# The score maxima of two pairs of heads taken in one visit, and two small steps moved to the second step of the experts' stage

## The chip, the cores and the metric

The kernel runs on one core of one Trainium2 chip. The metric is the device time of one execution in microseconds (us). Engines are named as in the profile: PE is TensorE, DVE is VectorE, ACT is ScalarE, POOL is GpSimd, SP issues the large DMAs.

## The reference

For each of 16 inputs x of 256 x 128 the result is `x + scan(xn) + experts(attention(xn))`, with `xn = layernorm(x)`:

```python
# branch one: a depthwise convolution and a state-space recurrence with 16 states
xf = depthwise_conv(xn, conv_w, conv_b)                       # 3 taps
dt = sigmoid(xf @ dt_w.T + dt_b) * (DT_MAX - DT_MIN) + DT_MIN
s  = exp(dt * A) * s + (dt * xf) * b ;  y = sum_d s * c        # along the 256 rows
# branch two: 16 heads of 64, causal attention with q and k scaled to length one
h = layernorm(xn) * g + b ;  q, k, v = h @ Wq, h @ Wk, h @ Wv
attn = softmax(where(causal, l2norm(q) @ l2norm(k).T * 10, -1e9))
h = layernorm((attn @ v) @ Wo) ;  gate = softmax(h @ gate_w + gate_b)
out = layernorm(sum_e gate[e] * (gelu(h @ w1[e] + b1[e]) @ w2[e] + b2[e]))   # 8 experts
```

## The kernel before

All weights stay in SBUF. The inputs go through a software pipeline written out by hand, one loop `body(i)` for each of the engines, which are joined by counting semaphores alone; every engine works through its own list strictly in order. `body(i)` has two stages. The **attention stage** has ten steps `k = 0..9`: scores, exponentials and weighted values of input i, the q, k, v projections of input i+1, the 16 state scans of input i (as far as `SCAN_AT` puts them here), layer norms of inputs i-1, i-2 and i+2. The **experts' stage** has ten steps `m = 0..9`: the output projection of input i, the eight experts of input i-1 (`expert_up`, `gelus`, `expert_down`, `add_expert`), and the preparation of input i+1: q and k are turned (`turn_qk`, eight transposes for two calls), split into a high and a low half (`high` on ACT, `low` on DVE), and a pass over the scores gives each row's maximum for the softmax.

That **max pass** is taken for one pair of heads at a time. On PE `scores_for_max(s, p)` writes four products of 64 rows each (L400, the two heads in the two halves of the array) and then adds the causal mask with four products of 128 rows (L404). On DVE `maxima(s, p)` reduces them with two `tensor_reduce` (L1101). All passes of inputs 1 to 15 use one double bank of PSUM, S2, so the pass of pair p waits until the maxima of pair p-1 are taken; passes stand in steps m = 1 to 8, one in each. `turn_max` (L420) turns four pairs' maxima, `copy_max` (L730) copies them.

PSUM has eight banks: S2, O2 and U2 of two banks each and J[0], J[1]. J takes the projections, `turn_qk`, `turn`, `turn_max` and `step_sizes`.

Other pieces that the change touches: `turn` (L335, L337) turns the normalised input i+2, `g_step(i+2, 6)` makes it (four normalisings, L1010), `g_step` 7 to 9 copy it out of PSUM and split it (L1035, L1036, L1040, L1043). `convolve` (L1175, L1179: three operations) gives `xf`, `step_sizes` (L575) multiplies it by dt_w, `step_tanh` (L767) and `step_inputs` (L1187, L1191) follow. `scan` and `add_state` (L1198, L1208) are one state of the recurrence. `turn_gate` (L523), `o_step` 14 (L1156), `gated_b2` (L529) and `o_step` 15 (L1159) hand the gates of input i-1 from PE to DVE and back twice before the first expert is added. POOL's `units` (L920) scale q and k to length one: four operations follow the last `norm_step` (L1066) in step m = 0, then `x_bias` (L935).

Of the kernel before, what the change touches and what calls it, by code (L numbers as in the profile page):

```python
# [14 lines left out]
P = 128  # L15
# [25 lines left out]
def build(nc, x, a_log, b, c, dt_w, dt_b, conv_w, conv_b, ln_g, ln_b, Wq, Wk, Wv, q_scale, k_scale,  # L41
          Wo, gate_w, gate_b, w1, b1, w2, b2, out):
    ctx = ExitStack()
    with ctx:
# [131 lines left out]
        J = [ctx.enter_context(nc.psum_tensor(f"J{n}", [P, 512], F32)) for n in range(2)]  # L176
# [48 lines left out]
        def max_bank(s, p):  # L225

            return O2 if s == 0 and p % 2 == 1 else S2
# [27 lines left out]
        def step_bank(s):  # L255
            return U[1][:, 0:SEQ] if s == 0 else J[1][:, 0:SEQ]

        TURN_AT = {0: 0, 1: 2, 3: 4, 4: 6}
        MAX_AT = {1 + p: (p,) for p in range(NP)}
# [65 lines left out]
        def _(pe):  # L325
            mm, tr = nc.tensor.matmul, nc.tensor.transpose

            def turn(s):
                pe.wait_ge(g_vec, s * KG + 10)
                if not isinstance(s, int) or s > 0:  # L330
                    pe.wait_ge(t_lo, s * NL - 1)
                if s == 1:
                    pe.wait_ge(mt_done, 1)
                for t in range(T):
                    tr(J[0][:, t * P:(t + 1) * P], xn[:, t, :], ident[:, :])  # L335
                for t in range(T):
                    last = tr(J[0][:, SEQ + t * P:SEQ + (t + 1) * P], z[:, t, :], ident[:, :])  # L337
                last.then_inc(g_tr, 1)
# [29 lines left out]
            def turn_qk(s, n):  # L368
# [6 lines left out]
                elif n < 2:  # L375
                    pe.wait_ge(qk_raw, NJ - 1 + n)
                else:
                    pe.wait_ge(t_lo, s * NL + n - 1)
                for a in range(2):
# [6 lines left out]
            def scores_for_max(s, p):  # L386

                pe.wait_ge(t_hi, s * NL + 2 * (p // 2) + 2)
                if p == 0:
                    from_one(pe, ex_done, s * NP)  # L390
                    from_one(pe, wo_copied, s)
                elif s == 0:
                    from_one(pe, mx_done, 2 * (p - 1))
                else:
                    pe.wait_ge(mx_done, s * 2 * NP + 2 * p)
                bank = max_bank(s, p)
                for t in range(T):
                    for a in range(2):
                        r = slice(a * DH, (a + 1) * DH)
                        mm(bank[:, a, t * P:(2 * t + 1) * P], QTh[r, p, t * P:(t + 1) * P],  # L400
                           KTh[r, p, 0:(t + 1) * P], start=True, stop=False, skip_group_check=True)
                for a in range(2):
# [4 lines left out]

            def turn_max(s, g):
                pe.wait_ge(mx_done, s * 2 * NP + NP * (g + 1))
                if g == 0:  # L410
                    if s == 0:
                        pe.wait_ge(t_lo, NL - 1)
                    elif s < LAST:
                        pe.wait_ge(g_vec, (s + 1) * KG + 12)
                    else:
                        pe.wait_ge(t_lo, (s + 1) * NL - 1)
                else:
                    pe.wait_ge(tanh_done, s + 1)
                for t in range(T):
                    last = tr(J[g][:, t * P:(t + 1) * P],  # L420
# [148 lines left out]
            def step_sizes(s):  # L569
# [3 lines left out]
                else:  # L573
                    pe.wait_ge(t_lo, (s + 1) * NL)
                mm(step_bank(s), dtwT[:, :], xf[:, :], start=True, stop=True).then_inc(dt_ready, 1)  # L575

            def prologue():
# [17 lines left out]
                for n in range(NL):  # L595
                    turn_qk(0, n)
                    if n % 2 == 1:
                        scores_for_max(0, n - 1)
                        scores_for_max(0, n)
# [10 lines left out]
            def body(i, older, old, new, newer):  # L610
# [24 lines left out]
                for m in range(NE + 2):  # L635
# [7 lines left out]
                    if new:  # L643
                        for p in MAX_AT.get(m, ()):
                            scores_for_max(i + 1, p)
# [17 lines left out]
                    if newer and m == 6:  # L663
                        turn(i + 2)
                    if new and m == 7:
                        step_sizes(i + 1)
# [15 lines left out]
        def _(act):  # L682
# [45 lines left out]
            def copy_max(s, g):  # L728
                act.wait_ge(mt_ready, 2 * s + g + 1)
                fn(mT[:, g, :], J[g][:, 0:SEQ], ACT.Copy).then_inc(mt_done, 1)  # L730
# [95 lines left out]
            def body(i, older, old, new, newer):  # L826
# [43 lines left out]
                for m in range(NE + 2):  # L870
# [10 lines left out]
                    if new and m > 0 and m in TURN_AT:  # L881
                        high(i + 1, TURN_AT[m])
                        high(i + 1, TURN_AT[m] + 1)
                    if old and 1 <= m < NE:
                        gelus(i - 1, m)
                    if new and m == 8:
                        step_tanh(i + 1)
# [106 lines left out]
        def _(dve):  # L994
# [18 lines left out]
            def g_step(s, n):  # L1013
# [18 lines left out]
                elif n == 7:  # L1032
                    dve.wait_ge(g_tr, s + 1)
                    from_one(dve, c_vec, (s - 1) * KC + 3)
                    V.tensor_copy(xnT[:, 1:SEQ + 1], J[0][:, 0:SEQ]).then_inc(g_vec, 1)  # L1035
                    V.tensor_scalar(hT[:, :], J[0][:, SEQ:2 * SEQ], lng, lnb, ALU.mult, ALU.add  # L1036
# [283 lines left out]
            G_AT = {0: (0, 1), 3: (2,)}  # L1320
            O_AT = {1: (5,), 3: (6, 7), 4: (8,), 5: (9, 10), 9: (12, 13)}
            O_LAST_AT = {2: (0, 1, 2), 3: (5,), 4: (6, 7, 8), 5: (9, 10), 7: (12, 13), 8: (14,), 9: (15,)}
            SCAN_AT = {1: (0,), 3: (1,), 5: (2,), 6: (3,), 8: (4,), 9: (5,)}
# [128 lines left out]
```

## Time and profile before

| | |
|---|---|
| median of three runs | 1122.25 us (1120.18 to 1125.5) |
| the profiled execution | 1120.17 us, its span 1118.4 us |
| PE busy | 1075.0 us, 96% |
| DVE busy | 959.6 us, 86% |
| ACT busy | 778.9 us, 70% |
| POOL busy | 277.7 us, 25% |
| granted TensorE clock, mean | 0.986 of full speed |

The span runs from the first instruction to the last. The time of the execution has 1.8 us outside it. One input takes 66.2 us in the middle of the run: the attention stage about 28.6 us and the experts' stage about 37.6 us. Matmuls overlap in the pipeline, so a matmul's own duration (0.27 us and the like) is longer than the distance from one start to the next (0.11 us).

### The profile page before, as it was taken

The page shows a single profiled execution, that of the slowest core. Times are in us where ns is not written, and L with a number is a line of the kernel's source. Part 1 is how long each engine was busy: PE and PEld are TensorE (multiplying, and loading weights), DVE is VectorE, ACT ScalarE, POOL GpSimd, SP SyncE. Part 2 cuts the span into 40 slices and gives each one's busy share as a digit, 9 for nine tenths or more (in the row PEclk, how much of TensorE's full clock was granted, in tenths as well). Part 3 has the DMA queues.
Part 4 walks back from the last instruction along what each step waited for, and adds up shares of the span by engine and source line. Part 5 has one row for each costly group of instructions (what it writes and reads, how often), then busy time and mean ns, then how long its engine had stood idle before and what let it go on. Part 6 is the DMA issues. An engine that isn't in the chain of part 4 may idle for free.

```text
span 1118.4 us, 27576 instructions
## 1 busy us (share of the span) xinstructions
PE 1075.0 (96%) x10435; PEld 912.2 (82%) x10435; DVE 959.6 (86%) x2543; ACT 778.9 (70%) x1772; POOL 277.7 (25%) x328
## 2 busy tenths in 40 slices
PE   4877999999999999999999999999999999999997
PEld 1664888888888888888888888888888888888897
DVE  8988798898988989898898989889898888988763
ACT  5873948668595876859677594867759587685653
POOL 2340314224031231404123140412403132140200
PEclk9995999999999999999999999999999999999999
DMA  7010000000000000000000000000000000000000
GB/s 210 7 39 10 2 11 7 1 16 1 11 7 11 6 2 16 1 11 6 6 11 2 11 7 11 6 1 16 2 11 6 11 7 6 6 6 1 7 2 10
DMA packets 18722, 14.60 MB, mean 13 GB/s; under 512 B 2408, under 2 KB 16160, under 8 KB 18592
## 3 DMA queue, kind: packets, MB, share of 16 engines
q1 hardware_dynamic: 17680, 12.76, 3.8%
q8 instruction: 84, 1.38, 0.5%
q14 instruction: 46, 0.38, 0.1%
q10 hardware_dynamic: 912, 0.09, 0.1%
HBM read 10.75 MB, written 2.10 MB: 11 GB/s over the span
## 4 chain that ended last, share of the span: by engine, by line
PE 89%; DVE 4%; issue 3%; ACT 2%; POOL 1%; SPq 0%; DMA 0%; POOLq 0%; DVEq 0%; ACTq 0%
PE O L565 19%; PE O L468 14%; PE S L484 5%; PE U L547 5%; PE U L548 5%; PE U L549 5%; PE J L382 5%; PE S L449 4%; PE J L343 4%; PE U L449 4%; PE S L404 4%; PE J L344 3%; PE J L345 3%; PE S L400 3%; PE O L475 2%
## 5 line engine op out<-in xcount | busy, mean ns | idle before, releaser
L777 ACT ACTIVATE hid<-U,b1c 128x256 f32<-128x256 f32 x512 | 200.5, 474 | 174.8 <-PE U L549 174.7
L565 PE MATMUL O<-w2s,hid 128*128 128x128 f32 x2048 | 251.1, 276 | 0.0
L565 PEld LDWEIGHTS O<-w2s,hid 128*128 128x128 f32 x2048 | 238.6, 192 | 2.9
L928 POOL TENSOR_SCALAR_AFFINE_SELECT P<-P 128x512 f32<-128x512 f32 x128 | 85.0, 664 | 618.6 <-ACT P L750 618.5
L468 PEld LDWEIGHTS O<-Vx,P 128*128 128x128 f32 x1536 | 188.0, 192 | 30.2 <-issue 14.3
L468 PE MATMUL O<-Vx,P 128*128 128x66 f32 x1536 | 188.6, 273 | 3.6 <-POOL P L928 2.0
L1198 DVE TENSOR_TENSOR_SCAN st<-aexp,u 128x256 f32<-128x256 f32 x256 | 178.8, 698 | 0.4 <-issue 0.3
L920 POOL TENSOR_TENSOR raw<-raw,nr 128x512 f32<-128x512 f32 x124 | 132.8, 1097 | 134.9 <-DVE nr L1066 134.9
L1208 DVE SCALAR_TENSOR_TENSOR y<-st,bc,y 128x256 f32<-128x256 f32 x240 | 133.5, 556 | 8.5
L547 PE MATMUL U<-h2h,w1h 128*128 128x256 f16 x480 | 130.9, 273 | 0.0
L549 PE MATMUL U<-h2h,w1l 128*128 128x256 f16 x480 | 130.9, 273 | 0.0
L548 PE MATMUL U<-h2l,w1h 128*128 128x256 f16 x480 | 130.9, 273 | 0.0
L1101 DVE TENSOR_REDUCE mxn<-S 128x2 f32<-128x256 f32 x248 | 125.7, 549 | 0.7 <-PE S L404 0.3
L762 ACT ACTIVATE aexp<-dt,negA 128x256 f32<-128x256 f32 x256 | 117.2, 518 | 0.0
L1169 DVE SCALAR_TENSOR_TENSOR acc<-O,gate,acc 128x128 f32<-128x128 f32 x240 | 73.1, 346 | 43.5 <-PE O L565 39.2
L1047 DVE TENSOR_REDUCE ssq<-sq 128x8 f32<-128x512 f32 x128 | 86.3, 674 | 0.5 <-ACT sq L701 0.4
L699 ACT ACTIVATE raw<-J 128x512 f32<-128x512 f32 x128 | 76.7, 599 | 3.1 <-PE J L345 3.1
L701 ACT ACTIVATE sq<-J 128x512 f32<-128x512 f32 x128 | 78.1, 610 | 0.0
L343 PE MATMUL J<-wh,hTh 128*128 128x512 f16 x188 | 72.8, 387 | 3.9 <-DVE hTl L1043 1.9
L344 PE MATMUL J<-wh,hTl 128*128 128x512 f16 x188 | 72.0, 383 | 0.0
L345 PE MATMUL J<-wl,hTh 128*128 128x512 f16 x188 | 71.9, 383 | 0.0
L382 PE MATMUL J<-ident,raw 128*128 128x128 f32 x512 | 68.6, 278 | 3.3 <-DVE raw L1075 2.1
(204 smaller groups left out, 2048.0 us busy)
## 6 DMA issues: line engine op xcount, KB each, us to landing
xin<-in_L_attn_x SPq DMA_DIRECT2D x16, 128.0 KB, 2.1
xres<-in_L_attn_x SPq DMA_DIRECT2D x16, 128.0 KB, 2.3
hid<-in_L_ffn_w SPq DMA_DIRECT2D x2, 1024.0 KB, 6.5
out_dram<-fin SPq DMA_DIRECT2D x16, 128.0 KB, 1.8
raw<-in_L_ffn_Wq SPq DMA_DIRECT2D x1, 512.0 KB, 4.7
raw<-in_L_ffn_Wk SPq DMA_DIRECT2D x1, 512.0 KB, 6.4
raw<-in_L_ffn_Wv SPq DMA_DIRECT2D x1, 512.0 KB, 7.4
wos<-in_L_ffn_Wo SPq DMA_DIRECT2D x1, 512.0 KB, 11.4
```

The source lines that it names most:

```text
L343: mm(dst, hi, wh[:, w0:w0 + 512], start=True, stop=False)
L382: last = tr(J[n % 2][:, (a * T + t) * P:(a * T + t + 1) * P], raw[:, chunk(t, kind, half), c0:c0 + P], ident[:, :])
L468: last = mm(dst, P32[:, p % 3, a, c0:c0 + P], Vx[:, kb, 2 * p + a, :], start=(kb == 0), stop=(kb == t))
L547: mm(dst, w1h[:, f:f + P], hi[:, :], start=True, stop=False)
L548: mm(dst, w1h[:, f:f + P], lo[:, :], start=False, stop=False)
L549: last = mm(dst, w1l[:, f:f + P], hi[:, :], start=False, stop=True)
L565: last = mm(O[e % 2][:, t * P:(t + 1) * P], hid[:, e % 2, m, t * P:(t + 1) * P], w2s[:, e * FC + m, :], start=(m == 0), stop=(m == FC - 1))
L777: fn(hid[:, e % 2, f % FC, :], U[q % 2][:, m * SEQ:(m + 1) * SEQ], ACT.Gelu_apprx_tanh, bias=b1c[:, f:f + 1], scale=1.0 / WS).then_inc(gel ...
L920: nc.gpsimd.tensor_tensor(group, group, nr[:, j * 8:(j + 1) * 8].unsqueeze(2).broadcast_to([P, 8, DH]), ALU.mult).then_inc(unit, 1)
L1101: V.tensor_reduce(mxn[:, t, g, hh:hh + DH + 2:DH + 1], max_bank(s, p)[:, :, t * P:(2 * t + 1) * P], AX.X, ALU.max, negate=True).then_inc(m ...
L1198: V.tensor_tensor_scan(st[:, d % 2, :], aexp[:, d, :], u[:, :], 0.0, ALU.mult, ALU.add).then_inc(scan_done, 1)
L1208: V.scalar_tensor_tensor(y[:, s % 2, :], st[:, d % 2, :], bc[:, d:d + 1], y[:, s % 2, :], ALU.mult, ALU.add).then_inc(y_done, 1)
```

## The change

- `scores_for_max` now takes two pairs in one call: products of pair p, products of pair p+1, masks of p, masks of p+1. The even pair lies in S2 and the odd one in J2 (the two J banks, now one tensor), for input 0 in O2. Calls stand in steps m = 2, 5, 6 and 7; `maxima` of both pairs follow in the same steps.
- `turn(i+2)` and `step_sizes(i+1)` move on PE from steps 6 and 7 to step 1, ahead of the expert's products, and use S2 where they used J. The first max pass waits until both have been read out of S2. `step_tanh` moves to step 1 on ACT. `turn_max` of the first half moves to U[0].
- `turn_qk` calls 4 and 5 (step 3) wait for the first two pairs' maxima, since these are now in the J banks.
- On DVE `g_step(i+2, 6)` moves to step k = 8 of the attention stage and the three `convolve` to k = 9; `g_step` 7 to 9 move to step m = 1. State 4's scan moves from k = 8 to k = 9, state 5's from k = 9 to m = 0. In m = 0 the scans of states 6 and 7 now stand behind `low` and the `norm_step`s, before them up to now.
- In body 0 attention takes seven scans where it took ten, and the experts' stage nine where it took six.

```diff
@@ -173,7 +173,8 @@
         O = [O2[:, n, :] for n in range(2)]
-        J = [ctx.enter_context(nc.psum_tensor(f"J{n}", [P, 512], F32)) for n in range(2)]
+        J2 = ctx.enter_context(nc.psum_tensor("J2", [P, 2, 512], F32))
+        J = [J2[:, n, :] for n in range(2)]
         U2 = ctx.enter_context(nc.psum_tensor("U2", [P, 2, 512], F32))
@@ -224,7 +225,14 @@
-            return O2 if s == 0 and p % 2 == 1 else S2
+            return S2 if p % 2 == 0 else O2 if s == 0 else J2
+
+        def turn_bank(s):
+            return J[0] if s < 2 else S2[:, 1, :]
+
+        def turned_max_bank(s, g):
+
+            return (U[0] if g == 0 and s > 0 else J[g])[:, 0:SEQ]
@@ -253,10 +261,10 @@
         def step_bank(s):
-            return U[1][:, 0:SEQ] if s == 0 else J[1][:, 0:SEQ]
+            return U[1][:, 0:SEQ] if s == 0 else S2[:, 0, 0:SEQ]
         TURN_AT = {0: 0, 1: 2, 3: 4, 4: 6}
-        MAX_AT = {1 + p: (p,) for p in range(NP)}
+        MAX_AT = {2: 0, 5: 2, 6: 4, 7: 6}
@@ -327,14 +335,15 @@
                 pe.wait_ge(g_vec, s * KG + 10)
-                if not isinstance(s, int) or s > 0:
-                    pe.wait_ge(t_lo, s * NL - 1)
                 if s == 1:
+                    pe.wait_ge(t_lo, NL - 1)
                     pe.wait_ge(mt_done, 1)
-                for t in range(T):
-                    tr(J[0][:, t * P:(t + 1) * P], xn[:, t, :], ident[:, :])
-                for t in range(T):
-                    last = tr(J[0][:, SEQ + t * P:SEQ + (t + 1) * P], z[:, t, :], ident[:, :])
+                elif s > 1:
+                    pe.wait_ge(ex_done, (s - 1) * NP)
+                for t in range(T):
+                    tr(turn_bank(s)[:, t * P:(t + 1) * P], xn[:, t, :], ident[:, :])
+                for t in range(T):
+                    last = tr(turn_bank(s)[:, SEQ + t * P:SEQ + (t + 1) * P], z[:, t, :], ident[:, :])
                 last.then_inc(g_tr, 1)
@@ -376,6 +385,8 @@
                     pe.wait_ge(t_lo, s * NL + n - 1)
+                if s > 0 and n in (4, 5):
+                    pe.wait_ge(mx_done, s * 2 * NP + 4)
                 for a in range(2):
@@ -383,41 +394,56 @@
-            def scores_for_max(s, p):
-
-                pe.wait_ge(t_hi, s * NL + 2 * (p // 2) + 2)
-                if p == 0:
-                    from_one(pe, ex_done, s * NP)
-                    from_one(pe, wo_copied, s)
-                elif s == 0:
-                    from_one(pe, mx_done, 2 * (p - 1))
-                else:
-                    pe.wait_ge(mx_done, s * 2 * NP + 2 * p)
+            def max_products(s, p):
                 bank = max_bank(s, p)
...
                            KTh[r, p, 0:(t + 1) * P], start=True, stop=False, skip_group_check=True)
+
+            def max_masks(s, p):
+                bank = max_bank(s, p)
                 for a in range(2):
...
+            def scores_for_max(s, p):
+
+                pe.wait_ge(t_hi, s * NL + p + 2)
+                if s == 0:
+                    from_one(pe, mx_done, 2 * (p - 1))
+                    max_products(0, p)
+                    from_one(pe, mx_done, 2 * p)
+                elif p == 0:
+                    pe.wait_ge(ex_done, s * NP)
+                    pe.wait_ge(wo_copied, s)
+                    pe.wait_ge(tanh_done, s + 1)
+                    if s < LAST:
+                        pe.wait_ge(g_vec, (s + 1) * KG + 12)
+                    pe.wait_ge(t_lo, s * NL + 4)
+                    max_products(s, p)
+                else:
+                    pe.wait_ge(t_lo, s * NL + NL)
+                    pe.wait_ge(mx_done, s * 2 * NP + 2 * p)
+                    max_products(s, p)
+                max_products(s, p + 1)
+                max_masks(s, p)
+                max_masks(s, p + 1)
+
             def turn_max(s, g):
...
                         pe.wait_ge(t_lo, NL - 1)
-                    elif s < LAST:
-                        pe.wait_ge(g_vec, (s + 1) * KG + 12)
                     else:
-                        pe.wait_ge(t_lo, (s + 1) * NL - 1)
-                else:
-                    pe.wait_ge(tanh_done, s + 1)
-                for t in range(T):
-                    last = tr(J[g][:, t * P:(t + 1) * P],
+                        from_one(pe, gelu_done, (s - 1) * NE * FC)
+                else:
+                    pe.wait_ge(t_lo, (s + 1) * NL)
+                for t in range(T):
+                    last = tr(turned_max_bank(s, g)[:, t * P:(t + 1) * P],
                               mxn[:, t, g, :], ident[:, :])
@@ -571,7 +597,7 @@
                 else:
-                    pe.wait_ge(t_lo, (s + 1) * NL)
+                    pe.wait_ge(wo_copied, s)
                 mm(step_bank(s), dtwT[:, :], xf[:, :], start=True, stop=True).then_inc(dt_ready, 1)
@@ -596,7 +622,6 @@
                         scores_for_max(0, n - 1)
-                        scores_for_max(0, n)
                     if n == 1:
@@ -640,9 +665,12 @@
                         turn_gate(i - 1, (i + 1) * NP)
-                    if new:
-                        for p in MAX_AT.get(m, ()):
-                            scores_for_max(i + 1, p)
+                    if new and m == 1:
+                        step_sizes(i + 1)
+                    if newer and m == 1:
+                        turn(i + 2)
+                    if new and m in MAX_AT:
+                        scores_for_max(i + 1, MAX_AT[m])
                     if old and 1 <= m < NE:
@@ -660,10 +688,6 @@
                         gated_b2(i)
-                    if newer and m == 6:
-                        turn(i + 2)
-                    if new and m == 7:
-                        step_sizes(i + 1)
                     if not old and m == NE + 1:
@@ -727,7 +751,7 @@
                 act.wait_ge(mt_ready, 2 * s + g + 1)
-                fn(mT[:, g, :], J[g][:, 0:SEQ], ACT.Copy).then_inc(mt_done, 1)
+                fn(mT[:, g, :], turned_max_bank(s, g), ACT.Copy).then_inc(mt_done, 1)
@@ -881,10 +905,10 @@
                         high(i + 1, TURN_AT[m] + 1)
+                    if new and m == 1:
+                        step_tanh(i + 1)
                     if old and 1 <= m < NE:
                         gelus(i - 1, m)
-                    if new and m == 8:
-                        step_tanh(i + 1)
                 if new:
@@ -1032,8 +1056,8 @@
                     from_one(dve, c_vec, (s - 1) * KC + 3)
-                    V.tensor_copy(xnT[:, 1:SEQ + 1], J[0][:, 0:SEQ]).then_inc(g_vec, 1)
-                    V.tensor_scalar(hT[:, :], J[0][:, SEQ:2 * SEQ], lng, lnb, ALU.mult, ALU.add
+                    V.tensor_copy(xnT[:, 1:SEQ + 1], turn_bank(s)[:, 0:SEQ]).then_inc(g_vec, 1)
+                    V.tensor_scalar(hT[:, :], turn_bank(s)[:, SEQ:2 * SEQ], lng, lnb, ALU.mult, ALU.add
                                     ).then_inc(g_vec, 1)
@@ -1317,11 +1341,11 @@
             E_AT = {0: (0, 1, 2), 2: (5, 6), 3: (7,)}
-            G_AT = {0: (0, 1), 3: (2,)}
+            G_AT = {0: (0, 1), 3: (2,), 8: (6,)}
             O_AT = {1: (5,), 3: (6, 7), 4: (8,), 5: (9, 10), 9: (12, 13)}
             O_LAST_AT = {2: (0, 1, 2), 3: (5,), 4: (6, 7, 8), 5: (9, 10), 7: (12, 13), 8: (14,), 9: (15,)}
-            SCAN_AT = {1: (0,), 3: (1,), 5: (2,), 6: (3,), 8: (4,), 9: (5,)}
-            FIRST_SCAN_AT = {1: (0, 1), 2: (2,), 3: (3,), 4: (4,), 5: (5,), 6: (6,), 7: (7,), 8: (8,), 9: (9,)}
+            SCAN_AT = {1: (0,), 3: (1,), 5: (2,), 6: (3,), 9: (4,)}
+            FIRST_SCAN_AT = {k: (k - 1,) for k in range(1, 8)}
@@ -1353,6 +1377,9 @@
                             g_step(i + 2, n)
+                    if new and k == 9:
+                        for n in range(3):
+                            convolve(i + 1, n)
                     if k != 6:
@@ -1364,46 +1391,42 @@
                         add_expert(i - 1, m - 2)
+                    if new and m in MAX_AT:
+                        maxima(i + 1, MAX_AT[m])
+                        maxima(i + 1, MAX_AT[m] + 1)
                     if old and m == 0:
-                        for d in (6, 7):
-                            scan(i, d)
-                            add_state(i, d)
+                        scan(i, 5)
+                        add_state(i, 5)
                     if new and m == 0:
...
                             norm_step(i + 1, 1, n)
+                    if old and m == 0:
+                        for d in (6, 7):
+                            scan(i, d)
+                            add_state(i, d)
                     if old and 2 <= m <= NE:
...
                         add_state(i, m + 7)
-                    if not old and 1 <= m <= 6:
-                        scan(i, m + 9)
-                        add_state(i, m + 9)
+                    if not old and m <= 8:
+                        scan(i, m + 7)
+                        add_state(i, m + 7)
                     if old and m == 1:
...
                         low(i + 1, TURN_AT[m] + 1)
-                    if new:
-                        for p in MAX_AT.get(m, ()):
-                            maxima(i + 1, p)
+                    if newer and m == 1:
+                        g_step(i + 2, 7)
+                        g_step(i + 2, 8)
                     if old and m == 1:
...
                         add_state(i, m + 7)
-                    if newer and m == 5:
-                        g_step(i + 2, 6)
-                    if new and m == 2:
-                        convolve(i + 1, 0)
-                    if new and m == 6:
-                        convolve(i + 1, 1)
-                        convolve(i + 1, 2)
+                    if newer and m == 1:
+                        g_step(i + 2, 9)
                     if not old and m == 3:
                         split_w1(1, 0, 1)
-                    if newer and m == 7:
-                        g_step(i + 2, 7)
-                        g_step(i + 2, 8)
-                    if newer and m == 8:
-                        g_step(i + 2, 9)
                     if new and m == 9:
```

## Rows read from the trace of the kernel before

**Rows 1.** The page, part 1: busy time and share of the span.
```profile
PE 1075.0 (96%) x10435; PEld 912.2 (82%) x10435; DVE 959.6 (86%) x2543; ACT 778.9 (70%) x1772; POOL 277.7 (25%) x328
```

**Rows 2.** Busy time by stretch; after POOL: granted clock, DMA share, GB/s.
```profile
18.00:42.00 24.00, 16.14 (x128) 8.85 (x127) 22.66 (x58) 17.70 (x35) 5.05 (x5) 1.00 0.47 135
81.00:106.00 25.00, 16.52 (x115) 10.95 (x116) 22.28 (x50) 5.82 (x10) 0.89 (x2) 0.50 0.04 11
464.63:502.21 37.58, 37.58 (x357) 33.64 (x356) 33.38 (x79) 22.25 (x53) 5.19 (x5) 1.00 0.03 9
502.21:530.82 28.61, 28.61 (x299) 23.03 (x299) 25.36 (x80) 25.54 (x58) 12.09 (x15) 1.00 0.02 6
```

**Rows 3.** Timeline of PE around step m = 2: start, us, what.
```profile
472.17 0.71 PE L529 MATMUL O<-b2s,gateT 8*128 8x128 f32 x4
472.80 2.05 PE L565 MATMUL O<-w2s,hid 128*128 128x128 f32 x16
474.79 0.34 PE L400 MATMUL S<-KTh,QTh 64*128 64x128 f16 x4
475.06 0.40 PE L404 MATMUL S<-maskb,identb 128*128 128x128 bf16 x4
475.29 0.27 PE L547 MATMUL U<-h2h,w1h 128*128 128x256 f16 x1
```

**Rows 4.** The chain that ended last, steps 6 and 7: start, us, what.
```profile
495.09 0.22 PE J L335 x2
...
499.23 0.43 PE J L575 x2
```

**Rows 5.** DVE's busy time in short stretches, each one piece of work.
```profile
459.91:461.63 1.72, 1.68 (x3) 1.00 0.00 0
463.61:464.73 1.12, 1.08 (x3) 1.00 0.00 0
466.97:468.35 1.38, 1.38 (x4) 1.00 0.00 0
468.35:468.99 0.64, 0.57 (x4) 1.00 0.00 0
472.12:473.05 0.93, 0.93 (x3) 1.00 0.00 0
474.97:475.50 0.53, 0.53 (x3) 1.00 0.00 0
490.31:491.33 1.02, 1.02 (x5) 1.00 0.00 0
494.01:494.95 0.94, 0.91 (x3) 1.00 0.00 0
497.71:498.89 1.18, 1.15 (x4) 1.00 0.00 0
```

**Rows 6.** Timeline of DVE, step k = 9 to step m = 1.
```profile
463.61 0.68 DVE L1198 TENSOR_TENSOR_SCAN st<-aexp,u 128x256 f32<-128x256 f32 x1
...
468.80 0.19 DVE L1066 SCALAR_TENSOR_TENSOR nr<-nw,ny 128x32 f32<-128x32 f32 x1
470.37 0.42 DVE L1156 COPY gateT<-O 128x256 f32<-128x256 f32 x1 [1.38 <-PE O L523]
```

**Rows 7.** Timeline of POOL: the first in the attention stage, the others m = 0.
```profile
66.11 2.42 POOL L920 TENSOR_TENSOR raw<-raw,nr 128x512 f32<-128x512 f32 x2
74.84 4.54 POOL L920 TENSOR_TENSOR raw<-raw,nr 128x512 f32<-128x512 f32 x4 [6.31 <-DVE nr L1066]
...
469.07 4.04 POOL L920 TENSOR_TENSOR raw<-raw,nr 128x512 f32<-128x512 f32 x4 [7.64 <-DVE nr L1066]
```

**Rows 8.** Timeline of DVE in body 0, beside the first two of rows 7.
```profile
66.71 0.99 DVE L1198 TENSOR_TENSOR_SCAN st<-aexp,u 128x256 f32<-128x256 f32 x1
67.73 1.08 DVE L1208 SCALAR_TENSOR_TENSOR y<-st,bc,y 128x256 f32<-128x256 f32 x1
...
75.40 1.08 DVE L1208 SCALAR_TENSOR_TENSOR y<-st,bc,y 128x256 f32<-128x256 f32 x1
```

## The prediction, made before the changed kernel was run

> **What bounds the kernel now.** I read the page first: PE is busy for 96% of the span, DVE for 86% [rows 1]. Then the windows of one input in the middle of the run: PE is busy in every moment of both stages, at full clock; DVE has 4.2 us to spare in the experts' stage and 3.3 us in the attention stage [rows 2]. So PE's own list sets the period of 66.2 us (37.58 + 28.61), and anything that PE no longer issues comes off it, once for each input. But DVE is only 11% behind, so the question of this change is whether DVE's new order still has each thing ready when PE asks. The third view is the timeline of the steps m = 0 to 3, where the change moves most.
>
> **What the change removes on PE.** In the timeline the last of the 16 matmuls of L565 starts at 472.80 + 2.05 - 0.28 = 474.57, the pass begins at 474.79, its masks at 475.06, the next product at 475.29 [rows 3]. Full-height matmuls start every 0.11 us, so going to 64-row products costs 0.22 - 0.11 = 0.1 us. The four products are two side-by-side couples of 128 and 256 columns: by PE's pace 0.055 + 0.11 = 0.165 us, but the masks come after 0.27 us, so going back costs 0.1 us as well. A single pass takes 0.50 + 0.1 = 0.6 us, two in one call 0.1 + 0.165 + 0.27 + 2 x 0.23 = 1.0 us. A joined call saves one way out and one way back, 0.21 us. Four for each input: **0.84 us**. The Trainium skill ("TensorEngine Tiling (Array Packing)", Key Properties) says that changing the tiling mode drains TensorE; it gives no figure, and the sum goes by the rows.
>
> `turn` (0.22 + 0.22 us) and `step_sizes` (0.43 us) [rows 4] only move: 0.87 us leave steps 6 and 7 and come into step 1. The same for every moved DVE operation. Nothing else on PE changes, no DMA does, and ACT (59% busy in this stage [rows 2]) only gets `step_tanh` earlier; its table load moves off the end, which PE did not wait for. With all else hidden, the 14 bodies that have an expert's stage and a next input (1 to 14) give 14 x 0.84 = 11.8 us.
>
> **DVE: is everything in time?** Prices, from one start to the next [rows 5]: scan with its add 1.12, the same beside POOL's `units` 1.72; a pair of `low` 1.38; the three norm steps 0.64; two reductions 0.93; `add_expert` 0.53; `g_step` 6 1.02; the last two convolutions 0.94, all three 1.34 with a first of `o_step` 14's size; `g_step` 7 and 8 1.18; `g_step` 9, `o_step` 14 and 15 about 0.35 each (copies of that size).
>
> Step k = 8: the four normalisings take the place of a scan that ran beside POOL. Uncovered they take 1.02 us, and if POOL holds them up by as much as it did the scan and its add (1.72 - 1.12), 1.6 us against 1.72: the same end within 0.2 us. After that DVE begins at 463.61 [rows 6]. Up to now scans 5, 6, 7 (3.36 us) stood before `low`; now convolutions and scans 4, 5 (1.34 + 2.24 = 3.58 us): `low` is 0.22 us later, at 467.2, and PE asks for it only behind eight transposes and the 32 matmuls of `output`, at 464.63 + 40 x 0.11 = 469.0. No cost.
>
> Then the norm steps end, and scans 6 and 7 follow where DVE sat idle for 1.38 us before `o_step` 14 at 470.37 [rows 6]. They begin at 467.2 + 1.38 + 0.57 = 469.15. Without any hindrance they end at 471.4.
>
> **The hindrance.** The last norm step releases POOL's four units, 4.04 us back to back [rows 7]. Up to now DVE had nothing with two SBUF inputs in that time. In body 0 it had one scan there: POOL's four then took 4.54 us in place of 4.04, and the add behind the scan 1.08 us in place of 0.48; in the attention stage a scan and an add that met the two units of 66.11 took 0.99 and 1.08 in place of 0.68 and 0.48 [rows 7, 8]. The numbers fit one reading: a DVE operation that meets a running unit does nothing until that unit ends, and then the next unit waits for it (the first unit ends at 66.11 + 1.04, the scan 0.55 us later at 67.70; the second ends at 68.53, the add 0.28 us later at 68.81). Played out from 469.15: scan 6 is first and holds unit 1 up until about 469.63 (of the 0.5 us that POOL lost in body 0 I give the scan 0.3, the add 0.2); unit 1 to 470.67, the add ends 470.95; unit 2 to 471.88, scan 7 ends 472.43 (0.88 late); unit 3 to 473.26, its add ends 473.54. So add, scan and add are late by 0.6 + 0.88 + 0.6 = **2.1 us**, and `o_step` 14 begins at 473.46. Bounds: from below nothing, if they slip through; from above the 2.1 us, since each of the three can meet one unit only. The rows show the add blocked outright and a scan blocked in part, so I take the upper end; were scan 7 to get in before unit 2, it is 1.2 us.
>
> The Trainium skill ("SBUF — State Buffer", Who interferes with whom) says that a DVE instruction with two SBUF inputs and a GpSimd instruction that reads SBUF exclude each other for the whole instruction. By it the hindrance is the 2.1 us; by the single blocked add alone it would be 0.6 us.
>
> **What PE then waits for.** In step 1 PE is ready for `gated_b2` at 472.17 + 0.87 - 0.6 = 472.44 (two moved pieces in, one pass out). It needs `o_step` 14, done at about 473.9: a stall of 1.5 us. Everything on PE behind it waits too, the first expert among them. PE reaches the double pass at 476.45 (`gated_b2` 0.63, L565 to the pass 1.99 less the way out [rows 3]) and, 1.0 + 12 x 0.11 + 16 x 0.11 later, `turn_qk` 4 at 480.55. That needs the maxima of both first pairs. DVE's list up to them has no gap: 473.46, `o_step` 14 0.36, `low` 1.38, `g_step` 7 and 8 1.18, scan 8 1.12, `g_step` 9 0.35, `o_step` 15 0.4, `add_expert` 0.53, four reductions 1.86: 480.7. Another 0.2 to 0.25 us. Thus 1.75 us of stall. In other words, without the hindrance DVE would be there at 478.7 and PE at 478.95: the slack is 0.3 us, the stall is the hindrance less 0.3, and the saving is used up once the hindrance is 1.15 us.
>
> Steps 5 to 9 cost nothing more: DVE has 0.53 + 1.86 + 1.12 = 3.5 us of work for each of the steps 5, 6, 7, of which PE takes 4.1, and the second pair's maxima are ready 1 us before the next call asks. Before, it had the same reductions there one at a time plus the moved work.
>
> For bodies 1 to 13: 1.75 - 0.84 = **+0.94 us each** (unrounded), 12.2 us. Body 14 has no `turn` and no `g_step` 7 to 9: PE is there 0.44 us sooner and the stall before `gated_b2` stays at 1.5, 1.5 - 0.84 = +0.7 us. Body 15 has no passes and the moved scan falls into idle time: 0. The prologue is paced by DVE and the saved 0.8 us of PE is not on the path: 0. Body 0: in 81 to 106 DVE is busy for 22.3 of 25 us and the PE clock is 0.50, the lower level, after PE idled [rows 2]; DVE gets three more scans there (3.4 us), loses convolutions and `g_step` 6 (2.4 us) and has 0.9 us more of hindrance, and its double calls wait for a slow PE pass in between. Bounds -1 (the passes wait less often) and +3; I take +1.
>
> Sum: 12.2 + 0.7 + 1 = 13.9 us. Against the profiled execution: 1120.17 + 13.9 = 1134.1 us. The median of the runs shown is 2.1 us (0.2%) above that execution, so 1136 against the median; I say **1135 us**, 1.1% slower. An error of 0.35 us in the stall is 5 us in all, so this case alone has 1128 to 1141.
>
> **The rivals.**
> *Faster.* DVE's scans are not held up by more than 0.3 us: the place is step m = 0 to 1, scans 6 and 7 beside L920. Then only the 0.84 us stands: 1120.2 - 11.8 = 1108.4, with body 0 and the base 1109. It decides below 1.15 us of hindrance. For it: PE has nothing else to wait for, and scans started before a unit run at 0.68. Against it: rows 7 and 8. Chance 0.21.
> *No change.* Scan 7 gets in ahead of unit 2: hindrance 1.2, stall 0.9, +0.06 us for each body; with body 0 about 1122. Or DVE comes earlier to step 1 than I reckon by the same 0.9 us. Chance 0.14.
> *Much slower.* PE's new idle time lets the granted clock fall to 0.50 as in body 0, where PE had been idle for over a third of 25 us [rows 2]. If each experts' stage ran 2 us at the lower level, of which half is lost, 14 bodies give 14 us more: about 1149. Against it: in 18 to 42 PE was busy for 16.1 of 24 us at clock 1.00, far emptier than 1.75 us in 37. Or more waits appear, at `turn_o` in k = 9 or `low` 5 in step 4, where slack is 0.2 us each. Chance 0.05.
> *The forecast.* 0.60.
>
> **How the numbers follow.** A measurement of this kernel can tell about 0.5% (5.6 us) from no change. Slower by more: the forecast less its low tail (0.57) and the much slower case, 0.62. Faster by more: the first rival, 0.21. Within: 0.17, the second rival and the forecast's tail. The range goes from 1110, inside the faster rival's spread, to 1141, the forecast's upper end; it leaves out some 0.18. As cases of both signs are in it, the likeliest one's own range is the 1128 to 1141 above.
>
> **What would show it.** In the changed kernel's profile the pass L400 to L404 x8 in one block, about 1.0 us; in step 1 PE idle before L529 for about 1.5 us, released by DVE's gateT (L1156 before); the adds of states 6 and 7 at 1.08 us and the scan of state 7 at 1.5 us, POOL's four units at about 5.4 us; no idle time before gateT; PE idle 0.2 us before the fifth `turn_qk`. Period 67.1 us. The prediction is wrong if the scans beside L920 keep 0.68 and 0.48 us, if DVE reaches `o_step` 14 before 472.4 in these terms, or if PE's idle time lies elsewhere.

## The result and the profile after

The changed kernel takes **1155.34 us** (median of 4 runs, 1154.8 to 1155.5) against 1121.28 us for the kernel before in the same comparison: ratio 1.0296, 95% interval 1.0268 to 1.0324. It is 3% slower, where 1.1% was forecast and 1141 us was the end of the range. The span grew from 1118.4 to 1153.6 us.

The page of the changed kernel, busy time first (it answers to [rows 1]), then the shares of the chain that ended last:
```profile
PE 1088.5 (94%) x10435; PEld 938.7 (81%) x10435; DVE 992.2 (86%) x2543; ACT 774.3 (67%) x1772; POOL 280.9 (24%) x328
...
PE 73%; DVE 15%; issue 8%; ACT 2%; POOL 1%; SPq 0%; DMA 0%; POOLq 0%; DVEq 0%; ACTq 0%
```
PE did the same 10435 matmuls, was idle for 22 us more, and took 13.5 us more of busy time for them: the joined passes save some 12 us of it, and a lower clock costs some 25. DVE, absent from the chain up to now but for 4%, holds 15% of it.

Whom PE waited for, in total, times, longest; then the same for one body, the one in which the clock did not fall (755 to 775 us, shown further below):
```profile
PE O L555 <- DVE gateT L1180: 19.1, 14, 1.8
```
```profile
PE O L555 <- DVE gateT L1180: 1.3, 1, 1.3
PE J L393 <- DVE mxn L1125: 0.2, 1, 0.2
```
The wait before `gated_b2` (L529 before, now L555) is new, once in each of the 14 bodies that the forecast named. DVE's timeline, steps 0 and 1, answers to [rows 6, 8]; below it POOL's four units (answers to [rows 7]):
```profile
482.71 0.19 DVE L1090 SCALAR_TENSOR_TENSOR nr<-nw,ny 128x32 f32<-128x32 f32 x1
482.82 0.68 DVE L1222 TENSOR_TENSOR_SCAN st<-aexp,u 128x256 f32<-128x256 f32 x1
483.54 1.08 DVE L1232 SCALAR_TENSOR_TENSOR y<-st,bc,y 128x256 f32<-128x256 f32 x1
484.54 1.52 DVE L1222 TENSOR_TENSOR_SCAN st<-aexp,u 128x256 f32<-128x256 f32 x1
486.10 1.08 DVE L1232 SCALAR_TENSOR_TENSOR y<-st,bc,y 128x256 f32<-128x256 f32 x1
487.11 0.41 DVE L1180 COPY gateT<-O 128x256 f32<-128x256 f32 x1
```
```profile
76.73 5.11 POOL L944 TENSOR_TENSOR raw<-raw,nr 128x512 f32<-128x512 f32 x4 [6.69 <-DVE nr L1090]
...
141.05 5.11 POOL L944 TENSOR_TENSOR raw<-raw,nr 128x512 f32<-128x512 f32 x4 [8.14 <-DVE nr L1090]
...
414.60 5.10 POOL L944 TENSOR_TENSOR raw<-raw,nr 128x512 f32<-128x512 f32 x4 [8.33 <-DVE nr L1090]
...
482.98 5.11 POOL L944 TENSOR_TENSOR raw<-raw,nr 128x512 f32<-128x512 f32 x4 [8.29 <-DVE nr L1090]
```
The add, the scan and the add take 1.08, 1.52 and 1.08 us where 0.48, 0.68 and 0.48 are their time alone. The idle time of 1.38 us before gateT is gone. From 414.60 to 482.98 is the period: 68.38 us, 2.2 us more than before.

What PE did next, in a body where the clock fell and in the one body of the 14 where it did not:
```profile
487.57 0.71 PE L555 MATMUL O<-b2s,gateT 8*128 8x128 f32 x4 [1.31 <-DVE gateT L1180]
488.21 3.24 PE L591 MATMUL O<-w2s,hid 128*128 128x128 f32 x16
491.38 0.50 PE L402 MATMUL S<-KTh,QTh 64*128 64x128 f16 x4
```
```profile
761.35 0.71 PE L555 MATMUL O<-b2s,gateT 8*128 8x128 f32 x4 [1.32 <-DVE gateT L1180]
761.98 2.05 PE L591 MATMUL O<-w2s,hid 128*128 128x128 f32 x16
763.97 0.34 PE L402 MATMUL S<-KTh,QTh 64*128 64x128 f16 x4
```
The same 16 matmuls take 3.24 us and not 2.05. The windows show the reason in their third column from the end, the granted clock:
```profile
486.00:487.57 1.57, 0.26 (x3) 0.00 (x0) 1.53 (x4) 1.21 (x4) 1.57 (x2) 1.00 0.00 0
487.57:491.00 3.43, 3.43 (x19) 3.31 (x20) 3.36 (x8) 0.00 (x0) 1.20 (x2) 0.69 0.13 38
```
In that second stretch part of the time is at full speed, 2.4 GHz, and part at half, 1.2 GHz. Up to 493.00 the granted clock is 0.69 as a mean over 5.43 us, so (1 - 0.69) x 5.43 = 1.7 us of full-speed clock are missing behind this wait. The time that it costs is less. In the body without the fall POOL's units begin at 756.75 and in the next body at 823.95, a period of 67.20 us; with the fall it is 68.38. So a fall costs **1.2 us of time**. The fifth `turn_qk` shows where the rest went: it starts 6.94 us after `gated_b2` without the fall (761.35 to 768.29), 0.17 us of that idle, and 8.16 us after it with the fall (487.57 to 495.73) and without idle time.

**The 35 us.** By POOL's lines, which begin in step 0 of each body: the changed kernel comes to body 0's units 1.9 us later (76.73 against 74.84), takes 1.1 us more for body 0, and 27.0 us more for bodies 1 to 13; what follows adds 5.1 us, of which body 14 up to the last attention stage makes 2.4. A steady body is 2.2 us longer, in two parts. 1.0 us stands also where the clock did not fall: 0.84 less for the joined passes, 1.32 and 0.17 us of waits, and 0.35 us that these three terms leave over. The other 1.2 us is the fall, in 12 of the bodies 1 to 13: 13 x 1.00 + 12 x 1.18 = 27.2.

### The profile page after: what moved, and what is told of

The parts are those of the page before. It is cut to its first block, busy times and chain, and to the rows that moved or that the text cites. A ratio compares the mean times of both kernels' runs of the same rounds, so it can differ in the third digit from the quotient of the medians.

```text
span 1153.6 us, 27541 instructions
## 1 busy us (share of the span) xinstructions
PE 1088.5 (94%) x10435; PEld 938.7 (81%) x10435; DVE 992.2 (86%) x2543; ACT 774.3 (67%) x1772; POOL 280.9 (24%) x328
## 3 DMA queue, kind: packets, MB, share of 16 engines
q8 instruction: 84, 1.38, 0.5%
## 4 chain that ended last, share of the span: by engine, by line
PE 73%; DVE 15%; issue 8%; ACT 2%; POOL 1%; SPq 0%; DMA 0%; POOLq 0%; DVEq 0%; ACTq 0%
PE O L591 20%; PE O L494 14%; DVE st L1222 5%; PE S L475 4%; PE U L475 4%; PE U L573 4%; PE U L574 4%; PE U L575 4%; PE J L352 3%; PE J L353 2%; PE J L354 2%; PE J L393 2%; PE O L501 2%; PE S L409 2%; PE S L402 2%
## 5 line engine op out<-in xcount | busy, mean ns | idle before, releaser
L591 PE MATMUL O<-w2s,hid 128*128 128x128 f32 x2048 | 265.2, 286 | 0.0
L591 PEld LDWEIGHTS O<-w2s,hid 128*128 128x128 f32 x2048 | 251.4, 200 | 2.9
L1222 DVE TENSOR_TENSOR_SCAN st<-aexp,u 128x256 f32<-128x256 f32 x256 | 190.5, 744 | 0.3 <-issue 0.3
L944 POOL TENSOR_TENSOR raw<-raw,nr 128x512 f32<-128x512 f32 x124 | 142.4, 1173 | 144.7 <-DVE nr L1090 144.7
L1232 DVE SCALAR_TENSOR_TENSOR y<-st,bc,y 128x256 f32<-128x256 f32 x240 | 138.2, 576 | 8.6
L1125 DVE TENSOR_REDUCE mxn<-S 128x2 f32<-128x256 f32 (+1 forms) x128 | 65.5, 554 | 11.6 <-PE S L409 10.9
L774 ACT ACTIVATE P<-S 128x768 f32<-128x768 f32 x64 | 51.9, 811 | 32.3 <-PE S L475 31.9
```

The costliest lines, as they stand in the source:

```text
L591: last = mm(O[e % 2][:, t * P:(t + 1) * P], hid[:, e % 2, m, t * P:(t + 1) * P], w2s[:, e * FC + m, :], start=(m == 0), stop=(m == FC - 1))
L944: nc.gpsimd.tensor_tensor(group, group, nr[:, j * 8:(j + 1) * 8].unsqueeze(2).broadcast_to([P, 8, DH]), ALU.mult).then_inc(unit, 1)
L1222: V.tensor_tensor_scan(st[:, d % 2, :], aexp[:, d, :], u[:, :], 0.0, ALU.mult, ALU.add).then_inc(scan_done, 1)
L1232: V.scalar_tensor_tensor(y[:, s % 2, :], st[:, d % 2, :], bc[:, d:d + 1], y[:, s % 2, :], ALU.mult, ALU.add).then_inc(y_done, 1)
```

## The experiments

Theory 1: DVE operations held up beside POOL's units make gateT late, PE idles, and the idle time itself lowers the clock. The rivals: DVE simply has too much to do; the clock falls because of the new passes or moved steps. "Clock 1.00 from 130 to 1000" below is the granted clock of that stretch, which holds the waits of bodies 1 to 13. Ratios are to the kernel before, with 95% intervals.

**Take the meeting away, leave DVE's order.** In POOL's list of the changed kernel:
```diff
                 if new:
+                    if old:
+                        pool.wait_ge(y_done, i * DS + 8)
                     for n in range(4):
                         units(i + 1, 1, n)
```


> The changed kernel with one wait more: POOL's four units of the second half begin only when DVE has finished the scans of states 6 and 7. Theory 1 (the three DVE operations beside POOL's units are late by 2.1 us, this makes PE idle 1.3 us before gated_b2, and this idle time makes the granted clock fall to 0.50 for 3.4 us, 1.7 us lost): adds 0.48 and scans 0.68 us in step 0, no idle time before L555, clock mean near 0.98; the units now lie beside step 1, so up to 0.9 us of waiting may come back before the fifth turn_qk; 1112 to 1130 us. Rival (DVE has too much work before gateT, whatever POOL does): idle time before L555 and 1155 us stay.

Measured: 1131.06 us, ratio 1.0072 (1.0046 to 1.0098).
```profile
477.33 0.68 DVE L1224 TENSOR_TENSOR_SCAN st<-aexp,u 128x256 f32<-128x256 f32 x1
478.05 0.48 DVE L1234 SCALAR_TENSOR_TENSOR y<-st,bc,y 128x256 f32<-128x256 f32 x1
478.45 0.42 DVE L1182 COPY gateT<-O 128x256 f32<-128x256 f32 x1
...
481.07 0.74 DVE L1066 CAST hTh<-hT 128x256 f16<-128x256 f32 x1
481.73 1.53 DVE L1224 TENSOR_TENSOR_SCAN st<-aexp,u 128x256 f32<-128x256 f32 x1
483.30 0.77 DVE L1234 SCALAR_TENSOR_TENSOR y<-st,bc,y 128x256 f32<-128x256 f32 x1
```
```profile
PE J L393 <- DVE mxn L1127: 9.0, 14, 1.7
...
PE O L591 <- ACT hid L801: 4.1, 13, 0.4
```
24 us come back, 1 us short of the range that was expected. Scan and add are at their own time again, and nobody waits before L555. But the units now meet the cast of `g_step` 8, scan 8 and its add, so 0.5 us return before the fifth `turn_qk`, and 0.3 us before the first expert's second product. PE's clock is 1.00 from 130 to 1000 us. The rival with too much work falls for the wait before `gated_b2`: the same list is in time there once POOL is out of the way.

**More work for PE in its idle time.** Before `gated_b2` (behind a wait for the bank's last reader, satisfied already), into a part of the bank that nobody reads:
```diff
+                        for _n in range(11):
+                            tr(O[0][:, 3 * P:4 * P], ident[:, :], ident[:, :])
                     if old and m == 1:
                         gated_b2(i - 1)
```


> The changed kernel with 11 transposes of the identity into an unused part of a PSUM bank, issued by PE between expert_up(1) and gated_b2, where it sat idle for 1.3 us: more work for PE, in the idle time. Theory 1 (the idle time makes the clock fall): clock stays at 1.00 in the steady bodies, some 1.7 us less for each of 13 or 14 bodies, 1130 to 1137 us. Rival (the clock falls because of the passes or of the two moved steps, not because of idle time): 1155 us or a little more.

> The changed kernel with 5 transposes in place of 11 between expert_up(1) and gated_b2: PE idles there for about 0.75 us and not for 1.3. The work and the releases are those of the kernel with 11. If a wait of 0.8 us leaves the clock alone, as in the kernel before with two scans moved, it takes the same 1136 to 1139 us as with 11. If any idle time in this place lowers the clock, 1150 us or more.

Measured: 1138.16 us with 11 transposes (ratio 1.0141, 1.0108 to 1.0174), 1139.41 with 5 (1.0136, 1.0119 to 1.0153). With 11, PE in one body:
```profile
479.10 1.36 PE L679 MATMUL O<-ident 128*128 128x128 f32 x11
480.58 0.71 PE L555 MATMUL O<-b2s,gateT 8*128 8x128 f32 x4
481.22 2.05 PE L591 MATMUL O<-w2s,hid 128*128 128x128 f32 x16
```
The work added some 17 us of matmuls (14 x 11 at 0.11 us), and the kernel is 17 us faster than the changed one. That is less than the 22 us of clock that were expected back (1137 us at most), and in line with 1.2 us of time for each fall. L591 is back at 2.05 us, the clock at 1.00 from 130 to 1000. With 5 transposes PE idles 0.77 us there, and the clock holds as well; in body 14, which has no `turn` in front, PE still idles 1.25 us, and there it falls. The period is 67.2 us in both: the same as in the changed kernel's body without the fall, and this is the kernel that the forecast described (67.1). The rival on passes and moved steps falls: both are in it.

**Let PE ask later.** `gated_b2` behind `expert_down` of step 1.

> The changed kernel with gated_b2 behind the first expert_down on PE, so that PE does not ask for gateT for 1.8 us more. Theory 1 in full (DVE's whole list up to the first maxima is late, not the gates alone): no idle time before L555, but 1.5 to 1.8 us before the fifth turn_qk instead; 1150 to 1157 us if that idle time lowers the clock too, about 1133 us if not. Rival (the gates are the only thing that is late): the idle time is gone for good, about 1110 us.

Measured: 1147.53 us, ratio 1.0228 (1.0199 to 1.0257).
```profile
487.87 0.34 PE L402 MATMUL S<-KTh,QTh 64*128 64x128 f16 x4 [1.26 <-DVE hT L1060]
488.04 0.34 PE L402 MATMUL J<-KTh,QTh 64*128 64x128 f16 x4
488.31 0.48 PE L409 MATMUL S<-maskb,identb 128*128 128x128 bf16 x4
488.59 0.63 PE L409 MATMUL J<-maskb,identb 128*128 128x128 bf16 x4
```
The wait moves on by one item, to `g_step` 7 ahead of the first pass, and not as expected to `turn_qk`; the time is below the 1150 us that was expected. The wait is 1.26 us, and the second masks already run at the lower clock (0.63 for 0.39 us). So the gates are only the first of the things that are late; DVE's list as a whole is.

**One part of the change in the kernel before.** Only this order on DVE, in step m = 0:
```diff
-                    if old and m == 0:
-                        for d in (6, 7):
-                            scan(i, d)
-                            add_state(i, d)
                     if new and m == 0:
                         low(i + 1, 0)
                         low(i + 1, 1)
                         for n in range(1, 4):
                             norm_step(i + 1, 1, n)
+                    if old and m == 0:
+                        for d in (6, 7):
+                            scan(i, d)
+                            add_state(i, d)
```


> The kernel before with one part of the change alone: on DVE the scans of states 6 and 7 stand behind low and the norm steps of step 0. Theory 1: the two adds take 1.08 us and the second scan 1.5 us, gateT is done at about 3.3 us later than before, PE idles about 1.5 us before gated_b2; with the clock falling after it +3.2 us for each of 14 bodies, about 1165 us; without a fall of the clock about 1142 us. Rival (joined passes and the steps moved into step 1 are needed for the loss): within 0.5% of 1121 us.

Measured: 1134.55 us, ratio 1.0104 (1.0076 to 1.0133).
```profile
475.27 1.08 DVE L1208 SCALAR_TENSOR_TENSOR y<-st,bc,y 128x256 f32<-128x256 f32 x1
476.27 1.52 DVE L1198 TENSOR_TENSOR_SCAN st<-aexp,u 128x256 f32<-128x256 f32 x1
477.83 1.08 DVE L1208 SCALAR_TENSOR_TENSOR y<-st,bc,y 128x256 f32<-128x256 f32 x1
```
```profile
479.30 0.71 PE L529 MATMUL O<-b2s,gateT 8*128 8x128 f32 x4 [0.83 <-DVE gateT L1156]
479.94 2.05 PE L565 MATMUL O<-w2s,hid 128*128 128x128 f32 x16
```
The same three durations to 0.01 us, with no other part of the change. The wait is 0.83 us where 1.5 was expected, and 11.3 us in all 14 bodies; the clock holds, and the time is below both that were expected. So this one reordering costs 1.0%.

**Idle time of PE by itself.** In the kernel with the scans later (next), where nothing is late, `gated_b2` of bodies 1 to 13 gets a wait, on `g_step` 8 or on scan 6:
```diff
+                    if old and newer and m == 1:
+                        pe.wait_ge(g_vec, (i + 2) * KG + 13)
                     if old and m == 1:
                         gated_b2(i - 1)
```


> The kernel with the scans later, and a wait put on PE: gated_b2 is not issued before DVE's g_step 8 is done, in bodies 1 to 13. Nothing else is late there, so this measures idle time of PE by itself; by the trace of the kernel without the wait it is about 1.0 us. If the clock holds as it did at 0.8 us: +1.0 us for each of 13 bodies, 1128 us. If it falls as at 1.3 us: +2.7 us each, 1150 us.

> The same with the wait on the scan of state 6, about 2.1 us of idle time. Theory 1 (idle time by itself lowers the clock, without joined passes late, scans beside POOL or DVE work that is behind): +2.1 us and +1.7 us for the clock, in 13 bodies, 1163 to 1168 us. Rival (the clock fell for another reason in the changed kernel): +2.1 us each, 1143 us.

Measured: 1127.83 us (ratio 1.0034, 1.0020 to 1.0048) and 1170.6 us (1.0405, 1.0374 to 1.0437). Waits of the first, then of the second, then the second's windows around one of them:
```profile
PE O L555 <- DVE hTh L1066: 12.8, 13, 1.0
```
```profile
PE O L555 <- DVE st L1224: 27.4, 13, 2.2
```
```profile
490.00:493.51 3.51, 1.41 (x13) 1.02 (x11) 3.44 (x8) 1.93 (x5) 2.91 (x4) 0.99 0.00 0
493.51:500.00 6.49, 6.49 (x37) 5.68 (x38) 2.06 (x6) 0.00 (x0) 0.00 (x0) 0.50 0.07 20
```
13 waits of 1.0 us cost 12.5 us by the medians, and 1.06 us each by POOL's periods (66.50 against 65.44): their own length and little more. 13 waits of 2.1 us cost 55 us, twice their length (27.4 us) and more than the 1163 to 1168 us that was expected; the rest is clock, at 0.50 for the 6.5 us behind this one. By turns the periods are 69.2 and 70.7 us, with a shorter and a longer stretch at 0.50. In two of the 13 bodies the clock did not fall, and the periods are 67.6 and 67.8 (all in the profiled execution, at 1163.4 us the shortest of four). So idle time alone does it: DVE is not late here, and nothing but the wait was put in.

**The scans later.** The changed kernel, with DVE's scans put where it has time:
```diff
-                    if old and m == 0:
-                        for d in (6, 7):
...
+                        for d in {2: (7,), 3: (8,), 5: (12,), 6: (13,), 7: (14,), 8: (15,)}.get(m, ()):
...
+                        for d in {1: (6,), 3: (9,), 4: (10, 11)}.get(m, ()):
```
The first dictionary stands ahead of `low`, the second behind `g_step` 8.

> The changed kernel with DVE's scans moved out of the tight stretch: state 6 behind g_step 8 in step 1, state 7 behind the first maxima, 8 and 9 in step 3, 10 and 11 in step 4, the rest as in the changed kernel. Nothing is taken away. Theory 1: no scan before gateT, so PE does not idle before gated_b2, the clock stays, and the 0.84 us of joined passes are left: period 65.4 to 65.6 us, 1110 to 1115 us. Rival (the scans take their time from PE wherever they stand): the idle time comes back before the fifth or the seventh turn_qk, 1125 us or more.

> The kernel with the scans later, but with the masks of each pair straight behind its products, so that PE goes from 64-row to 128-row products and back twice in each call. Both theories of the loss say the same here; it measures the term that was to be saved: 0.21 us for each call, 0.84 us for each input, so 10 to 13 us more than the kernel with joined passes. If a call is no cheaper joined, the times are equal.

Measured: **1115.32 us**, ratio 0.9913 (0.9893 to 0.9933); with the passes unjoined 1125.01 us, 1.0006 (0.9991 to 1.0021). POOL's lines give the periods, joined first:
```profile
468.81 4.04 POOL L944 TENSOR_TENSOR raw<-raw,nr 128x512 f32<-128x512 f32 x4 [8.30 <-DVE nr L1090]
...
534.24 4.04 POOL L944 TENSOR_TENSOR raw<-raw,nr 128x512 f32<-128x512 f32 x4 [8.29 <-DVE nr L1090]
```
```profile
473.96 4.05 POOL L944 TENSOR_TENSOR raw<-raw,nr 128x512 f32<-128x512 f32 x4 [8.29 <-DVE nr L1090]
...
540.26 4.05 POOL L944 TENSOR_TENSOR raw<-raw,nr 128x512 f32<-128x512 f32 x4 [8.29 <-DVE nr L1090]
```
65.43 against 66.30 us: joining saves 0.87 us for each input. By the medians it is 9.7 us in all, at the lower edge of the 10 to 13 expected; against the 66.20 us of the kernel before, the kernel with the scans later gains 0.77 us. No steady body waits any more, and DVE does all that it did.

**Body 0 as well.** ACT's second `split_w1` behind `high` 2 and 3, DVE's scan 8 of body 0 behind `g_step` 8.

> The kernel with the scans later, and body 0 mended too: ACT turns to the second half of w1 only after high 2 and 3, and DVE takes state 8's scan behind g_step 8. PE idled 4.1 us there before the first pass and the clock was at 0.50 for 27 us after it. Theory 1: the idle time becomes about 2 us shorter; 1 to 4 us less than the kernel with the scans later, 1111 to 1114 us, if the clock falls there all the same. If DVE is the bound of that stage whatever the order, the same 1115 us.

Measured: 1112.44 us, ratio 0.9895 (0.9877 to 0.9914). PE's wait before the first pass of body 0 fell from 4.1 to 2.1 us, but 1.3 us of it came back before the next `turn_qk` (3.04 for 1.71), and the clock falls there all the same. This is the fastest of the kernels, 1% below the kernel before; against the one without this edit the difference of 2.9 us is near what the runs scatter.

## Why the prediction was wrong, point by point

- **Joined passes save 0.84 us.** Right: 0.87 for joining alone.
- **Moved pieces fit, DVE in time at k = 8 and for `low`.** Right: no wait appears there.
- **Three operations late by 2.1 us.** Right in kind and size: 0.60 + 0.84 + 0.60 = 2.04. The bound from above was the value, and POOL lost 1.07 us (5.11 for 4.04; I had it at about 5.4).
- **Wait of 1.5 us before `gated_b2`, 0.25 more before `turn_qk`.** Right in place, a little too long: 1.31 and 0.17. The second shows only in the body where the clock did not fall and vanishes where it did, since PE is slower than DVE there.
- **+0.94 us for each steady body.** 1.0 where the clock holds, and that is in part luck. The waits are 0.26 us shorter than the 1.75 forecast, and the 0.35 us that the terms leave over made up for it. A part of the latter is that a wait costs a little more than its idle time (1.06 us for 0.97 in the kernel with a wait of 1 us); the rest is open.
- **Body 0: +1.** Right: 1.1.
- **The step that failed: the clock.** The sum had no term for it. "Much slower", in which PE's idle time lets the clock fall, got the chance 0.05, and I set it aside because PE had been "far emptier" in 18 to 42 at clock 1.00. That compared busy shares of long stretches. In the experts' stages the length of one gap told the cases apart:

| idle time of PE, us | kernel | gaps | followed by clock 0.50 |
|---|---|---|---|
| 0.8 | changed, 5 transposes | 13 | 0 |
| 0.8 | before, two scans behind | 14 | 0 |
| 1.0 | scans later, wait on `g_step` 8 | 13 | 0 |
| 1.25 to 1.33 | changed, `gated_b2` behind `expert_down` | 13 | 12 |
| 1.3 to 1.4, last 1.8 | changed | 14 | 13 |
| 2.1 | scans later, wait on scan 6 | 13 | 11 |

The fall cost 1.2 us of time in each of 13 bodies, 15 us. The rival's own price, 14 us, was nearly right; its chance was not. The forecast's 1134.1 and these 15 us make 1149, and the experiments without the fall stand at 1138 and 1139.

- **The rest, 5 us.** In the changed kernel's profile the clock also fell in the prologue (0.94 from 18 to 45 us) and in the last attention stage (0.87 from 1080 to 1106). The first gives the 1.9 us ahead of body 0, the second the 2.7 us behind body 14. The kernel before has 1.00 in the prologue and in its own last attention stage (1050 to 1076) in its profiled execution. The first is not the change's: the kernel with only DVE's two scans moved has the prologue of the kernel before, and its clock fell there too; the kernel with waits of 2.1 us has the prologue of the changed one, its clock held, and it comes to body 0's units at 74.89 us, as the kernel before does (74.84). In the last attention stage the 10 us ahead of the fall (at 1086.2 us) hold no gap of PE over 0.57 us, but two of 0.57 and 0.56 us, 2.3 us apart; so the length of one gap is not the whole rule. Why the clock falls there, and why in some executions only, stays open.

## What to carry to other kernels

Before work on SBUF tiles is put into DVE's idle time, look at what POOL does in those microseconds: 2.24 us of scans became 4.3 beside POOL, and moving them by one step or more made a loss of 3% a gain of 0.9%. Where TensorE is the bound, price a new wait by its length and by what the clock does behind it. Against the 65.4 us of the kernel with the scans later, a body with a wait of 1.0 us took 1.1 us more; a body of the changed kernel, with 1.3 us before `gated_b2`, took 1.8 us more at full clock and 3.0 where it fell. A wait that cannot be avoided can be filled with matmuls that nobody needs, as here with 5 or 11 transposes.

## What the runs showed of the hardware that I had not expected

Eleven useless transposes in each of 14 bodies made the changed kernel 17 us faster. A gap of 1.3 us was not always followed by the lower clock: at 761.35 it was not, and of the gaps of 1.35 us that both kernels have in the prologue, the one in the kernel before left the clock at 1.00 and the one in the changed kernel was followed by passes at half speed. After 2.1 us idle the clock cost nothing in two bodies (periods of 67.6 and 67.8 us), 1.6 us in some and 3.1 in others (69.2 and 70.7 us by turns), with the same work behind.

The Trainium skill ("SBUF — State Buffer", Who interferes with whom) says that the one that starts first keeps the port for its whole instruction. The runs agree, and add that the two took turns: three DVE operations and four of POOL's, back to back, alternated one by one (DVE's three begin at 483.54, 484.54 and 486.10 us, POOL's second and third at 484.30 and 485.48), each DVE operation losing 0.6 to 0.84 us and POOL's four 1.07 us in all.
